# The opening of a vision-transformer tower: two statistics steps and six input loads in another order

## The reference

```
z = _layernorm(patches, ln1_g, ln1_b)                 # patches: (64, 36, 768)
z = jnp.einsum('bnp,pe->bne', z, W_proj) + b_proj     # (64, 36, 256)
z = _layernorm(z, ln2_g, ln2_b)
z = jnp.concatenate([cls, z], axis=1) + pos_emb       # (64, 37, 256)
...
h = h + attention(_layernorm(h))                      # one head of 256, own token masked
h = h + experts(_layernorm(h))                        # 8 experts, top 2, capacity, layernorm
```

## Time and profile before

| what | value |
|---|---|
| median of 3 runs (lowest, highest) | 421.92 us (421.41, 422.31) |
| the profiled execution's own time | 423.82 us |
| its span, first to last instruction | 421.4 us |
| PE busy in the span | 349.8 us, 83% |
| DVE, ACT, POOL busy | 316.3, 259.0, 240.4 us |
| granted clock of PE, mean over the span | 0.909 |

### The profile page before, as it was taken

How to read it: one execution, slowest core, us unless ns; L and a number is a source line. 1 busy time by engine, 2 the same in 40 slices (tenths; PEclk the granted TensorE clock), 3 DMA queues, 4 the chain that set the end, 5 groups by cost and what they waited for, 6 DMA issues and landing times. The chain is left out here.

```text
span 421.4 us, 8094 instructions
## 1 busy us (share of the span) xinstructions
PE 349.8 (83%) x2190; PEld 312.1 (74%) x2190; DVE 316.3 (75%) x868; ACT 259.0 (61%) x548; POOL 240.4 (57%) x434
## 2 busy tenths in 40 slices
PE   2689999999999999660024999999999999999940
PEld 0478889999899997450013899999999999999930
DVE  7665878788777865868888555778787878787772
ACT  3336677778777785445700478686868686868520
POOL 4156888778778876310004433248686868654574
PEclk9989999999999999955555699999999999999995
DMA  6632043544535398658703587467777777752221
GB/s 185 194 64 64 2 109 109 148 135 125 145 117 144 100 121 150 169 164 239 5 0 87 154 213 192 149 155 209 209 213 206 213 207 212 206 177 56 65 76 54
DMA packets 49278, 58.38 MB, mean 139 GB/s; under 512 B 12167, under 2 KB 38007, under 8 KB 49244
## 3 DMA queue, kind: packets, MB, share of 16 engines
q1 hardware_dynamic: 42602, 43.11, 39.4%
q0 software_dynamic: 5568, 14.09, 12.7%
q10 hardware_dynamic: 1074, 0.79, 0.6%
HBM read 36.74 MB, written 21.36 MB: 138 GB/s over the span
## 5 line engine op out<-in xcount | busy, mean ns | idle before, releaser
L944 PE MATMUL pz<-halves 128*128 128x448 f32 x384 | 90.4, 372 | 0.0
L961 PE MATMUL pall<-halves 128*128 128x448 f32 x384 | 89.7, 369 | 0.8 <-DVE halves L1334 0.8
L944 PEld LDWEIGHTS pz<-halves 128*128 128x128 f32 x384 | 73.7, 192 | 6.1
L961 PEld LDWEIGHTS pall<-halves 128*128 128x128 f32 x384 | 71.1, 189 | 6.8 <-DVE halves L1334 1.1
L1573 POOL DMA_INDIRECT held<-x_rows,gidx x32 | 33.8, 1057 | 65.3 <-DVE gidx L1276 41.2
L712 ACT ACTIVATE wproj<-pz,b1t 128x448 f32<-128x448 f32 x64 | 40.7, 636 | 47.1 <-PE pz L944 41.3
L1334 DVE TENSOR_TENSOR halves<-wproj,halves 128x448 fp32r<-128x448 f32 x64 | 40.2, 628 | 30.5 <-ACT halves L724 25.0
L829 PE MATMUL pall<-halves 128*112 128x256 f32 x396 | 52.5, 287 | 4.6 <-DVE halves L1055 4.6
L1482 POOL TENSOR_TENSOR rs<-rs,neghalf 112x1 f32<-112x1 f32 x88 | 50.2, 570 | 7.3
L829 PEld LDWEIGHTS pall<-halves 128*112 128x112 f32 x396 | 48.1, 177 | 5.0 <-DVE halves L1055 2.7
L1598 POOL DMA_INDIRECT out<-rows,didx x28 | 37.2, 1330 | 25.6 <-DVE rows L1382 15.9
(11 more groups left out here) (265 smaller groups left out, 716.7 us busy)
## 6 DMA issues: line engine op xcount, KB each, us to landing
stage<-in_w SPq DMA_DIRECT2D x32, 512.0 KB, 5.0
stage<-in_x SPq DMA_DIRECT2D x64, 108.0 KB
x_rows<-x SPq DMA_DIRECT2D x22, 224.0 KB, 2.8
x_rows<-held SPq DMA_DIRECT2D x22, 224.0 KB, 4.2
sums<-rows SPq DMA_DIRECT2D x7, 448.0 KB
out<-held SPq DMA_DIRECT2D x21, 111.0 KB
x_rows<-zero SPq DMA_DIRECT2D x1, 1474.9 KB
wproj<-in_w_proj ACTq DMA_DIRECT2D x1, 768.0 KB
```

What stands on the lines that cost most here:

```text
L944: m = nc.tensor.matmul(bank(k % 2)[:, 0:SLOTS], w[:, c, k * 128:(k + 1) * 128], xs[:, e % 2, c, :], start=(n == 0), stop=(n == 3 * EC - 1))
L961: m = nc.tensor.matmul(pall[:, 2 * (e % 2) + o, 0:SLOTS], w[:, k, o * 128:(o + 1) * 128], hs[:, k % 2, :], start=(k == 0 and n == 0), stop ...
```

## The change

Three things move; none is added or removed. In DVE's order, statistics of tile 1 come right after the low part of the projection, ahead of the five instructions of the bias row. `low_x(0)` comes between the first and the second of those five. Statistics of tile 2 stay behind the bias row. In SP's order, the six transfers of input tiles 2 and 3 come ahead of the eight attention loads.

```diff
@@ sync: behind the loads on c_g
+            for t in range(2, 4):
+                sp.wait_ge(s_xz, t + 1)
+                load_x(t, t)
             load(c_a, wq[:, :, :], wq_t.rearrange("(c p) o -> p c o", p=128))
...
             load(c_a, rbb[:, :], rep(router_b, 0, P))
-
-            for t in range(2, 4):
-                sp.wait_ge(s_xz, t + 1)
-                load_x(t, t)
@@ vector: behind the low part of the projection
+            stats_x(1, 1)
+            aggr_x(1)
             dve.wait_ge(c_pe, 1)
             V_.tensor_copy(zb[:, :], bank(2)[0:2, 0:ED]).then_inc(c_zb, 1)
+            low_x(0)
             dve.wait_ge(c_zb, 1)
...
                 .then_inc(c_dve, 1)
-
-            low_x(0)
-            for t in range(1, 3):
-                stats_x(t, t)
-                aggr_x(t)
+            stats_x(2, 2)
+            aggr_x(2)
```

## The result

The change made the kernel slower: 424.32 us (422.28 to 425.44, 21 executions) against 422.18 us (421.13 to 423.67, 21 executions), ratio 1.0037 with a 95% interval of 1.0026 to 1.0049. The medians differ by 2.1 us; the ratio makes 1.6 us (1.1 to 2.1). That much was lost where 1.5 us gained had been forecast, and it is outside the range. In two of the rounds one disturbed execution of the kernel before, of 616 and of 1216 us, is left out.

The account below looks back on a forecast made before the run. PE was taken to bound the kernel once its pipeline filled; z(1) 0.15 us sooner plus 1.48 us of clock made 1.6 us, from a 421.92 us median to 420.3, put at 420.4 us, range 419.2 to 421.9.

Parts of the forecast that it names:

- DVE's steps: DVE's opening: tile 1 statistics at 12.0, `zbias` ending at 16.1, then tile 2 statistics; z(1) allowed at 21.3, 1.5 us sooner.
- if only this had changed, nothing would be won: DVE's reordering ahead of tile 2: 2.95 us saved on tile 1 all but lost to the later z(0).
- 1.25 us of statistics: Tile 1 statistics put ahead of `zbias` on DVE; with PE's wait for `zbias`, z(0) starts 1.1 us later.
- the clock: PE's opening: lower clock moves from z(1) onto z(0) and `turn_x(1)`; 1.6 us won, 420.4 us, chance 0.38.
- the credit: Lower clock on z(1) in the traced kernel before, counted as costing 1.48 us, to be won when it moves.
- the price: Lower clock on z(0) and `turn_x(1)` in the changed kernel, counted as costing 1.48 us there.
- the start of z(0): PE starts z(0) at 16.25 instead of 15.14, 1.1 us later, waiting for `zbias`, which ends at about 16.1.
- my case: Lower clock after the 3.3 us hole ahead of z(0): z(1) starts at 22.65, 1.6 us won in all, chance 0.38.
- The landing of the weights: Attention weights behind the moved tile loads in SP's queue: `c_a` 2.2 us later, at 20.7, between 20.5 and 21.9.
- the sum: Start of z(1) on PE after the late weights and their transposes: 21.8 instead of 22.81, 1.0 us gained.
- The slower rival: Moved loads hold `c_a` beyond 21.7; at 22.6, z(1) starts 0.9 us later, 422.8 us; chance 0.07.
- the lower clock on both z(0) and z(1): PE slowed on both products in the opening: 0.1 us won instead of 1.6; counted within the 0.07 for slower.

Follow-up runs that it names:

- the changed kernel with all three additions: Changed kernel with 37-row loads cut in two, thirteen idle products at PE's start, ten ahead of z(0), four ahead of z(1): 420.37 us, ratio 0.9958 to before.
- the filled kernel: Changed kernel plus ten unread idle products on PE ahead of z(0) and eight ahead of its wait for the attention weights: 422.21 us, ratio 1.0001 to before.
- The filled kernels: Kernels with unread idle products in PE's holes; ratios to before: DVE's part 0.9994, whole change 1.0001, SP's part 0.9986, kernel before 0.9990.
- the filled kernel before: Kernel before plus seven unread idle products on PE ahead of z(0) and eight ahead of z(1): 422.12 us, ratio 0.9990 to before.

## Why the prediction was wrong

**Right.** DVE's steps: statistics of tile 1 at 12.0 without a wait (12.08), no wait for tile 2 of note (none to 0.29 us), the hole ahead of z(0) longer (3.1 us for the 3.3 predicted). `turn_x(1)` came directly behind z(0). That "if only this had changed, nothing would be won" was right too, and too mild.

**Right by the wrong reason.** The later z(0) was put down to the "1.25 us of statistics" ahead of `zbias`. By the prediction's own numbers `low_x(0)` could not start before 13.72 in any case, and `zb` would have been done by then without the statistics or with them. The 1.1 us are the four instructions of the bias row that now stand behind `low_x(0)` and no longer run while ACT writes the high part. In the trace DVE had 1.6 us of idle time around `zb`.

**The step that failed is the clock.** It was put as: "If it now comes after the hole of 3.3 us, it hits z(0) and `turn_x(1)`: 1.48 us [...] but what follows runs at full clock: in all 0.15 + 1.48 = 1.6 us." Three things in it were wrong.

First, the credit. The 1.48 us that the stretch on z(1) cost in the traced execution were taken for a cost of before in every one. Of three traces of before one has the stretch there. In another it lies on z(0), where the wait for tile 2 until 19.7 us hid it, and L858 starts at 26.3 in both of the others. My base was an execution that took 1.6 us more than the median. The prediction said so ("not every run need have had the lower clock at 24 us") and took off 0.1 us for it, where it should have taken off nearly all.

Second, the price. From the start of z(0) to the transposes of the weights the prediction counted 1.48 us more than at full clock. This part ran from 17.66 to 22.15, 16.66 to 22.11 and 17.97 to 23.73 in the three traces, against 3.23 us at full clock (15.87 to 19.10 in the trace of the changed kernel with all three additions): 1.3, 2.2 and 2.5 us more. In two of them the lower clock held for 6.8 us and covered z(0) whole, 4.18 us instead of 2.35. And the wait for tile 2, which hid a slow z(0) before, is what the change removed. The cover went as the need for it grew. It isn't the whole of it: with DVE's part alone the wait for tile 2 is still there, until 19.47 in its trace, and the loss is no smaller.

Third, "what follows runs at full clock": one of the three traces of the changed kernel has a second stretch, on z(2). So has one of before.

**A term that was off beside it** is the start of z(0), 16.25 predicted and 17.66, 16.66 and 17.97 measured. The prediction took the bias products from the traced execution, where the twelve of them took 4.07 us, the shortest of the six traces:

```profile
7.66 4.07 PE L751 MATMUL pall<-wproj,ln1bb 128*2 128x256 f32 x12 [7.66 <-DVE ln1bb L1037]
```

In the others they took up to 5.28 us. Before, this too was covered by tile 2; in the changed kernel it moves z(1). In the first trace of the changed kernel z(0) started 1.4 us later than predicted, and z(1) came 1.4 us later than the 22.65 of my case.

What the runs show in its place: in the changed kernel the lower clock holds for 6.8 us of the opening on the mean of three traces, against 3.4 before, most of it on z(0) and what follows at once, and a slow z(0) is no longer covered. With idle products in PE's holes the loss of 1.6 us is gone (ratio 1.0001, from 0.7 us under before to 0.8 over), the instructions being otherwise the same.

**Mis-sized.** The landing of the weights: predicted 2.2 us later, between bounds of 2.0 and 3.4; measured 3.5 in the trace and 2.7 in SP's part alone. I had taken the lower end. With the clock held up z(1) stood at 22.5, in the trace of the filled kernel, instead of the 21.8 of the sum. Cutting the loads made the weights 2.7 us earlier and changed nothing in the time as it was.

**The slower rival** was given 0.07, by a late landing of the weights; the loss came by another mechanism, which I had in the text only as "the lower clock on both z(0) and z(1)", with a gain of 0.1 us left. That sum too stood on the untypical base.

What stays open: how the two parts share their loss (2.3 and 1.3 alone, 1.6 together), by which hole SP's part loses, and what the removed wait for tile 2 is worth. No run moves the statistics alone or `low_x(0)` alone; that the place of `low_x(0)` makes the hole is read from the traces. The filled kernels hold about 3 us more at the upper clock than before does and are not faster by it. In the traces of two of them that time lies in the routing (54.6 us at the lower clock between 160 and 260 us, instead of 61.4), and 58.0 us stand there in two unfilled traces of before, so it differs from execution to execution and says little of the opening.

## What to carry to other kernels

Before one trace's rare feature is given a price, see whether it is in other executions: here the first two traces showed a gain of 0.3 us and the medians a loss of 2.1. In an opening where PE mostly waits, count the length of each hole of PE and not only what ends it. Where PE waits for two results, see which of the two can be made while another engine works at the other: here the order that put both in a row made the hole 0.9 us longer. A wait that is removed elsewhere may be what had covered a slow stretch. A mean clock over the whole span doesn't tell where the lower clock lay; read it by stretches. And look at what is queued ahead of a load that lands late: three loads of 37 rows, cut into 36 and 1, made 2.6 us in the landing of the last weight.

## What the runs showed of the hardware

- In the stretches before the first change of level the profile gives PE's clock as 1.00, but twelve product records of L751 took 4.07, 4.40 and 5.28 us in three traces of before, and 2.75 us behind thirteen products at the start. Products of the same shape thus took up to 1.9 times as long; so they ran partly or wholly at the lower level (1.2 GHz), which that column does not show. The Trainium skill says that the idle state is the slow one (TensorE: Matmul & The Clock Gate, The HAM clock gate); the products agree, the column does not.
- The clock can fall onto PE in the midst of work that counts as busy. In the filled kernel before:

```profile
30.04 3.14 PE L835 MATMUL pall<-halves 128*112 128x256 f32 x18
```

  This z(2) follows 7 us of PE without a hole, of which 1.84 us were products of one column. Six of the eighteen traces of this case have a slow z(2) at this place (3.10 to 3.68 us instead of 2.35), twelve have not.
- The same program, launched again, has its stretches at the lower clock in other places: on z(1), on z(0), or on z(2) in three traces of before, with spans of 421.4, 419.4 and 420.6 us.
